# One DRAM row per token and choice for the expert results, in place of accumulating scatters

## The reference

```
scores = softmax(x @ Wg.T)                       # 16 experts
topi = the best 4 experts out of the best 2 of 4 groups
y = sum over the 4 chosen e of scores[e] * (silu(x @ W1[e].T) * (x @ W3[e].T)) @ W2[e].T
z = (silu(x @ Ws1.T) * (x @ Ws3.T)) @ Ws2.T      # shared expert
out = x_residual + y + z
```

## Time and profile before

| | |
|---|---|
| median of 3 runs | 1341.67 us (1340.03 to 1342.01) |
| the profiled execution | 1353.53 us, span 1351.8 us |
| PE busy | 1150.4 us, 85% of the span |
| DVE, POOL, ACT busy | 876.2 us, 688.8 us, 541.6 us |
| granted TensorE clock, mean | 0.936 |
| DMA traffic | 169.84 MB, mean 126 GB/s |
| expert loop of FFN f, of FFN h | about 460 to 651 us, about 1119 to 1317 us |
| seam after FFN f | about 651 to 760 us |
| end after FFN h | 1317 to 1351.8 us |

### The profile page before, as it was taken

One profiled execution on the slowest core, in us unless ns is written; L12 is line 12 of the kernel. 1 busy time (PEld: TensorE's weight loads), 2 busy tenths in 40 slices (PEclk: granted clock), 3 DMA queues, 4 the chain that ended last, 5 costly groups with the idle time before them and its releaser, 6 DMA issues.

```text
span 1351.8 us, 26055 instructions
## 1 busy us (share of the span) xinstructions
PE 1150.4 (85%) x8706; PEld 615.6 (46%) x8706; DVE 876.2 (65%) x2067; ACT 541.6 (40%) x846; POOL 688.8 (51%) x841
## 2 busy tenths in 40 slices
PE   6888999998898899999287899999879878899990
PEld 2343444442654556566144344444247445565650
DVE  5578898991674345555389799999667524354543
ACT  2124777779520122222032477777844011222210
POOL 4352344444036577767453355454520656667671
PEclk9887999999988999999689899999998988899995
DMA  4424333320824679887745322121053347788868
GB/s 140 147 86 126 111 116 120 109 65 3 287 83 131 183 164 161 151 159 108 191 138 169 117 57 58 55 60 52 3 211 87 108 149 180 133 148 157 156 87 262
DMA packets 145875, 169.84 MB, mean 126 GB/s; under 512 B 20240, under 2 KB 130768, under 8 KB 145232
## 3 DMA queue, kind: packets, MB, share of 16 engines
q1 hardware_dynamic: 115856, 128.79, 32.8%
q0 software_dynamic: 29184, 38.36, 16.8%
q10 hardware_dynamic: 704, 1.02, 0.2%
HBM read 93.29 MB, written 76.18 MB: 125 GB/s over the span
## 4 chain that ended last, share of the span: by engine, by line
PE 57%; DVE 18%; DMA 7%; issue 6%; ACT 6%; SPq 2%; another core or an unknown queue 2%; POOL 2%; POOLq 0%; ACTq 0%; DVEq 0%
PE pair_ps L1992 10%; PE o_ps L1757 9%; ACT arena L845 4%; DVE nm L1119 4%; PE pair_ps L2025 4%; DMA x_slots<-y_sb,slot_i 4%; DVE bm L1119 3%; PE pair_ps L2028 2%; PE t_ps L1783 2%; PE pair_ps L1707 2%; PE pair_ps L1588 2%; PE pair_ps L1687 2%; PE pair_ps L1999 2%; PE pair_ps L1712 2%
## 5 line engine op out<-in xcount | busy, mean ns | idle before, releaser
L845 ACT ACTIVATE arena<-pair_ps 128x1024 f32<-128x1024 f32 x320 | 322.8, 1024 | 131.0 <-PE pair_ps L1682 76.1
L625 POOL TENSOR_SCALAR_AFFINE_SELECT arena<-arena 128x512 f32<-128x512 f32 (+1 forms) x320 | 174.9, 547 | 240.9 <-ACT arena L845 240.4
L1119 DVE TENSOR_REDUCE nm<-pair_ps 128x2 f32<-128x1024 f32 (+1 forms) x192 | 232.6, 1222 | 33.4 <-PE pair_ps L1731 29.6
L685 POOL DMA_INDIRECT x_slots<-y_sb,slot_i x128 | 123.9, 968 | 168.4 <-DVE slot_i L1317 89.9
L1757 PE MATMUL o_ps<-arena 128*9 128x512 f32 (+7 forms) x2048 | 177.0, 441 | 4.1 <-POOL arena L625 3.9
L1992 PE MATMUL pair_ps<-arena 128*128 x512 | 167.7, 469 | 2.4 <-ACT arena L896 2.4
L1119 DVE TENSOR_REDUCE bm<-pair_ps 128x8 f32<-128x1024 f32 x128 | 155.4, 1218 | 4.2 <-PE pair_ps L1731 1.0
L701 POOL DMA_INDIRECT y_h<-xnT,dest x80 | 125.3, 1566 | 53.5 <-DVE xnT L1476 25.2
L701 POOL DMA_INDIRECT y_f<-xnT,dest x80 | 124.6, 1558 | 44.6 <-issue 20.5
L1459 DVE TENSOR_TENSOR arena<-arena,pair_ps 128x128 f32<-128x128 f32 x144 | 41.4, 288 | 124.7 <-ACT arena L901 70.0
L1992 PEld LDWEIGHTS pair_ps<-arena 128*128 128x128 f32 x512 | 93.7, 194 | 43.6 <-issue 6.0
(11 more groups left out here) (275 smaller groups left out, 1999.7 us busy)
## 6 DMA issues: line engine op xcount, KB each, us to landing
arena<-x_slots SPq DMA_DIRECT2D x128, 132.5 KB
arena<-in_w SPq DMA_DIRECT2D x4, 2816.0 KB, 18.6
arena<-q_a SPq DMA_DIRECT2D x64, 96.0 KB
arena<-q_b SPq DMA_DIRECT2D x64, 96.0 KB
y_f<-hw SPq DMA_DIRECT2D x11, 512.0 KB, 2.9
y_h<-hw SPq DMA_DIRECT2D x11, 512.0 KB, 2.9
arena<-in_w SPq DMA_DIRECT2D x2, 2048.0 KB, 17.2
arena<-y_f SPq DMA_DIRECT2D x8, 512.0 KB
```

Of the source, the lines that this page charges most:

```text
L625: pool.affine_select(p, p, pattern, ALU.is_ge, 0.0, base=0, channel_multiplier=-1)\
L685: pool.indirect_dma_start(x_slots, bass.IndirectOffsetOnAxis(ap=slot_i[:, t, k:k + 1], axis=0), y_sb[:, t, :], None).then_inc(sm(f"scat{n ...
L845: act.activation(p_ring[:, U % RING, :], pair_ps[:, pair_at("T", n, u)].rearrange("p a c -> p (a c)"), ACT.Exp, scale=SCALE).then_inc(sm(" ...
L1119: dve.tensor_reduce(dst, src, X, ALU.max, negate=not 2 <= u < 4).then_inc(sm("t_max_done"), 1)
```

## The change

- There is one DRAM tensor for each FFN, `y_rows[f]`, with a row for each pair of token and choice (8192 rows of 256 floats) and 1024 spare rows for padding. A result tile is scattered by one plain indirect DMA, with no `compute_op`. The wait for the scatter three before and the second scatter of a mixed tile are gone: 72 scatters in each FFN.
- A row of `x_slots` carries four destination rows in place of one token number (268 floats in place of 265). `where` reads weight and destination by one multiplication and one reduction, in four DVE instructions per four tiles in place of six and more.
- `store_x` and the 22 clearing DMAs are gone; only the clearing of the empty slots stays. The residual stays in `x_sb`.
- Behind the loop SP loads the four rows of each token, two tiles (1 MB, runs of 4 KB) a DMA: 8 DMAs with 8.4 MB, before 12 with 6.3 MB. The last two reuse the buffer of the first two and wait until DVE has summed tiles 0 to 3.
- `dve_sum` adds the four rows of two tiles and `x_sb` in three instructions: 1024, 512 and 512 elements per partition. `pool_back` is gone, so DVE does all of it.
- The output is stored in eight pieces of 256 KB.

```diff
-ACCS = 3
+Y_ROWS = ROWS * TOPK + P * XR
...
-            def store_x(b):
-                sp.wait_ge(sm("e_z_free"), TB * (b + 1) + past(f, NT))
-                sp.dma_start(y_acc[f][0][b * T:(b + 1) * T, :].rearrange("(t p) e -> p t e", p=P),
-                             x_sb[:, b * TB:(b + 1) * TB, :]).then_inc(sm("acc_x"), 16)
...
-            sp.wait_ge(sm("store_second"), 16 * MIXED * (1 + past(f, 1)))
+            rows = y_rows[f][0:ROWS * TOPK, :].rearrange("(t p k) e -> p t k e", p=P, k=TOPK)
             for b in range(B):
-                for a, to in ((0, x_sb), (1, back), (2, back2)):
-                    rows = y_acc[f][a][b * T:(b + 1) * T, :].rearrange("(t p) e -> p t e", p=P)
-                    sp.dma_start(to[:, b * TB:(b + 1) * TB, :], rows).then_inc(sm(f"load{2 * b + a % 2}"), 16)
+                if b == B - 1:
+                    sp.wait_ge(sm(f + "_x"), TB)
+                for u in (0, 2):
+                    sp.dma_start(back[b][:, u:u + 2], rows[:, b * TB + u:b * TB + u + 2])\
+                        .then_inc(sm(f"load{2 * b + u // 2}"), 16)
...
-            for b in range(B):
-                sp.wait_ge(sm("h_x"), (b + 1) * TB)
-                sp.dma_start(out_d[:, b * TB:(b + 1) * TB, :], x_sb[:, b * TB:(b + 1) * TB, :]).then_inc(sm("stored"), 16)
+            for t in range(0, NT, 2):
+                sp.wait_ge(sm("h_x"), t + 2)
+                sp.dma_start(out_d[:, t:t + 2, :], x_sb[:, t:t + 2, :]).then_inc(sm("stored"), 16)
...
             def result_out(j):
                 pool.wait_ge(sm("e_dest"), j // 4 + 1 + past(f, NJ // 4))
                 pool.wait_ge(sm("e_y_ev"), j + 1 + past(f, NJ))
-                if j == 0:
-                    pool.wait_ge(sm("acc_x"), 16 * B * (1 + past(f, 1)))
-                scatter_out(outs.index((j, 0)))
-                if j in MIX:
-                    scatter_out(outs.index((j, 1)))
+                pool.indirect_dma_start(y_rows[f], bass.IndirectOffsetOnAxis(ap=dest[:, j:j + 1], axis=0),
+                                        yt[:, j % XR, :], None).then_inc(sm(f"store{j % XR}"), 16)
...
+        def dve_sum(dve, f, q):
+            b, u, t = q // 2, q % 2 * 2, 2 * q
+            done = q + 1 + past(f, 2 * B)
+            part = back[b][:, u:u + 2]
+            dve.wait_ge(sm(f"load{q}"), 16 * (loads(q) + past(f, loads(q))))
+            dve.tensor_tensor(part[:, :, 0:2, :], part[:, :, 0:2, :], part[:, :, 2:4, :], ALU.add).then_inc(sm("back_half"), 1)
+            dve.wait_ge(sm("back_half"), done)
+            dve.tensor_tensor(part[:, :, 0, :], part[:, :, 0, :], part[:, :, 1, :], ALU.add).then_inc(sm("back_sum"), 1)
+            dve.wait_ge(sm("back_sum"), done)
+            dve.tensor_tensor(x_sb[:, t:t + 2, :], x_sb[:, t:t + 2, :], part[:, :, 0, :], ALU.add).then_inc(sm(f + "_x"), 2)
```

More of the change, by code:

```diff
@@ L185, in build @@
         y_flat = y_sb[:, :, :].rearrange("p t e -> p (t e)")
-        back = arena[:, o_p:o_p + NT * E].rearrange("p (t e) -> p t e", t=NT)
-        back2 = arena[:, o_p + NT * E:o_p + 2 * NT * E].rearrange("p (t e) -> p t e", t=NT)
+        back = [part.rearrange("p (u k e) -> p u k e", u=TB, k=TOPK) for part in
+                (arena[:, o_p:o_p + T * 8], arena[:, o_p + T * 8:o_p + T * 16], y_flat[:, 0:T * 8], arena[:, o_p:o_p + T * 8])]
         sil = sb("sil", [P, 2, T])
@@ L226, in build @@
         k_d = {s: nc.dram_tensor("k_" + s, (B, BLOCKS[s] - 2, 3, P, T), BF16).ap() for s in "ab"}
-        y_acc = {f: [nc.dram_tensor(f"y_{f}{a}", (ROWS + 4 * P, E), F32).ap() for a in range(ACCS)] for f in "fh"}
+        y_rows = {f: nc.dram_tensor(f"y_{f}", (Y_ROWS, E), F32).ap() for f in "fh"}
         pair_ps = ctx.enter_context(nc.psum_tensor("pair_ps", [P, RINGP, 2, 512], F32))
@@ L245, in build @@
         o += 16
-        nowhere = c_f[:, o:o + XR]
-        rows_i = c_f[:, o + XR:o + XR + NT]
-        o += XR + NT
+        rows_i = c_f[:, o:o + NT * TOPK].rearrange("p (t k) -> p t k", t=NT)
+        nowhere = c_f[:, o + NT * TOPK:o + NT * TOPK + XR]
+        o += NT * TOPK + XR
         lane, lane_late, lane_unit = c_f[:, o:o + 1], c_f[:, o + 1:o + 2], c_f[:, o + 2:o + 3]
@@ L499, in sp_ffn_slots @@
             sp.wait_ge(sm("e_order"), 1 + past(f, 1))
-            for b in range(B - 1):
-                store_x(b)
             sp.wait_ge(sm("padded"), 16 * NE * (1 + past(f, 1)))
@@ L637, in pool_combine @@
             pool.tensor_tensor(osq[:, n % 2], yv, yv, ALU.mult).then_inc(sm("b_sq"), 1)
-        def pool_back(pool):
-            pool.wait_ge(sm("back_sum"), TB)
-            for t in range(TB, NT):
-                if t % TB == 0:
-                    for q in (2 * (t // TB), 2 * (t // TB) + 1):
-                        pool.wait_ge(sm(f"load{q}"), 16 * loads(q))
-                pool.tensor_tensor(back[:, t, :], back[:, t, :], back2[:, t, :], ALU.add).then_inc(sm("back_sum"), 1)
         def pool_out_bias(pool, t):
@@ L653, in pool_out_bias, with pool_k_ones @@
             pool.tensor_tensor(x_sb[:, t, :], x_sb[:, t, :], bo[:], ALU.add).then_inc(sm("a_bo"), 1)
+        def pool_k_ones(pool):
+            pool.memset(arena2[:, 16 * T // 2:], ONES2).then_inc(sm("k_ones"), 1)
         def pool_attn(pool, s):
-            pool.memset(arena2[:, 16 * T // 2:], ONES2).then_inc(sm("k_ones"), 1)
             for b in range(B):
@@ L732, in _ @@
             pool.wait_ge(sm("a_ones"), 1)
+            pool_k_ones(pool)
             pool_attn(pool, "a")
             pool_ffn(pool, "f")
-            pool_back(pool)
             vo = v_all.rearrange("p g t (h c) -> p g t h c", h=2)
@@ L1228, in dve_seam, with dve_back @@
                 dve_seam_rstd(dve, 1 if s == "a" else 3, a, c)
-        def dve_back(dve, f, t):
-            if t % TB == 0:
-                for q in (2 * (t // TB), 2 * (t // TB) + 1):
-                    dve.wait_ge(sm(f"load{q}"), 16 * (loads(q) + past(f, loads(q))))
-            if f == "h" or t < TB:
-                dve.tensor_tensor(back[:, t, :], back[:, t, :], back2[:, t, :], ALU.add).then_inc(sm("back_sum"), 1)
-                dve.wait_ge(sm("back_sum"), t + 1 + past(f, NT))
-            else:
-                dve.wait_ge(sm("back_sum"), t + 1)
-            dve.tensor_tensor(x_sb[:, t, :], x_sb[:, t, :], back[:, t, :], ALU.add).then_inc(sm(f + "_x"), 1)
-            if f == "f":
-                dve.wait_ge(sm("f_x"), t + 1)
-                dve_stats(dve, 2, t)
+        def dve_sum(dve, f, q):
[8 more added lines that the diff above has]
+            dve.tensor_tensor(x_sb[:, t:t + 2, :], x_sb[:, t:t + 2, :], part[:, :, 0, :], ALU.add).then_inc(sm(f + "_x"), 2)
+        def dve_back(dve, t):
+            if t % 2 == 0:
+                dve_sum(dve, "f", t // 2)
+                dve.wait_ge(sm("f_x"), t + 2)
+            dve_stats(dve, 2, t)
         def dve_ffn(dve, f):
@@ L1537, in _ @@
             dve_ffn(dve, "h")
-            for t in range(NT):
-                dve_back(dve, "h", t)
+            for q in range(2 * B):
+                dve_sum(dve, "h", q)
         def pe_turn(pe, s, b, u):
```

81 lines of the change are left out of this document (23 added, 58 removed).

## The result

The change took 1390.63 us (median of 4 runs, 1371.99 to 1406.57) beside 1340.85 us before (4 runs, 1337.96 to 1342.01): 1.026 of before, 95% interval 1.019 to 1.034. I had forecast 1337.0 us and a range of 1327.0 to 1345.5. The sign was wrong, and the range missed it by 45 us.

What follows compares the result with a forecast made beforehand. PE was taken to bound the expert loops, DVE the seam, DMA and DVE the end. Start of the loops -1.5, seam -0.9 and end -2.3 made -4.7 us: 1348.8 profiled, 1337.0 us for the median, range 1327.0 to 1345.5.

Steps and rivals of the forecast that it cites:

- start of the loops: Start of the expert loops: without the fourth store, loads of tiles 4 and 5 come sooner; -1.5 us in f, 0 in h.
- Rival A: Expert loops: heavy DMAs cause the stalls seen in loop h, half of them go, -6 us more, 1331 us; chance 0.22.
- my account of the loop: Expert loop: it follows PE, which hides cheaper scatters, fewer `where` instructions and less DMA traffic, so these are worth nothing.
- tail behind the loop, f and h: Behind each expert loop: the last scatters start and land sooner, so SP's first load comes 4.2 us (f), 4.3 us (h) earlier.
- first issue to first sum, f: First landing behind loop f: the first sum waits for 1.05 MB in place of 1.57, 5.1 us after issue, -1.7 us.
- a sum of two tiles, at the end: DVE's three adds for two tiles: 1.2 + 0.69 + 0.69 = 2.6 us; eight of them at the end take 20.8 us.
- end of loop f to first L999, seam of block b: Seam behind loop f: tail, landing and unstretched DVE instructions outweigh longer sums, so the first L999 comes 6.0 us earlier.
- seam behind the first load, to the scatters of h: Seam on DVE between the FFNs: -0.9 us with its tail, bounds -2.6 and +1.7; longer sums against less stretching by POOL.
- end, from the first load: Last loads, sums and output stores: 29.1 us against 27.1 before, +2.0, on a start 4.3 us earlier, so -2.3.
- Rival C: Seam: POOL's contention goes on, the relief of 4.4 us fails and stretched adds cost 3.8 more; +3.5, 1345.2 us; chance 0.14.
- rival B: Loads at the end stay at 350 GB/s, so the end is +0.8 in place of -2.3; 1340.1 us; chance 0.10.
- Rival D: Landing and stores give nothing: plain scatters land as late as accumulating ones, PE's wait at the start stays; 1340.1 us; chance 0.09.

Runs made afterwards that it cites:

- before_row268: Kernel before with rows of 268 in place of 265 floats, the extra ones repeating the token's row: 1331.13 us (0.999) without stalls, 1403.77 us (1.029) with stalls.
- change_again: The change itself, unaltered, measured again beside the kernel before in a session without stalls: 1316.75 us, 0.987 of before.

## Why the prediction was wrong, and where it was right

**The step that failed.** "Cheaper scatters, fewer DVE instructions in `where` and less DMA traffic lie beside PE there and are worth nothing, as long as PE's work hides them" was argued from the loop and tacitly used for the stage in front of it. Apart from the -1.5 us for the fourth store, the scatter phase was not in the sum, in either direction, and the wider row was not costed. In the measurement that the forecast was held against, this stage cost 41.9 us (23.6 in f, 18.3 in h) and the loops behind it 10.9. The runs show both sides of it:

Without stalls the stage is bound by the scatters. The page of the change (second session), chain that ended last, by line:

```profile
PE pair_ps L1943 11%; PE o_ps L1708 9%; DMA x_slots<-y_sb,slot_i 8%; ACT arena L806 4%; DVE nm L1080 4%; PE pair_ps L1976 4%; DVE bm L1080 3%; PE pair_ps L1979 3%; PE t_ps L1734 2%; PE pair_ps L1658 2%; PE pair_ps L1638 2%; PE pair_ps L1663 2%; PE pair_ps L1950 2%; PE pair_ps L1539 2%; PE pair_ps L1633 2%
```

8% of the span is a wait for scatters into x_slots, as in seven other profiles without stalls (10 to 12% in the three with pauses, none listed for three in flight), and 4% in the profile that I predicted from. PE is through with the shared expert and waits for rows, here the kernel before with rows of 268 floats and the change:

```profile
451.77 0.66 PE L1967 MATMUL t_ps<-c_f,arena 128*128 128x128 f32 x2 [7.24 <-DMA arena<-x_slots]
```

```profile
448.68 0.41 PE L1918 MATMUL t_ps<-c_f,arena 128*128 128x128 f32 x2 [3.06 <-DMA arena<-x_slots]
```

"The first three stores end before PE is through with the shared expert, so they go at nothing; DVE and PE hide them" is the mis-sized term: no engine is seen waiting for the stores, but the scatters beside them end later, and the loop's first loads wait for the scatters. I had priced the start of the loops at -1.5 us. By the stages of profiles without stalls (the kernel with rows of 268 floats, 84.6 / 81.9, against the change, 78.9 / 79.7) it is -7.9, from one execution each in two sessions; by the times of one session the stores are worth 3.4 us in the kernel before and 6.0 in the change. In my trace of before its own stalls (ACT waited 9.57 and 9.99 us at 422.21 and 432.80) kept PE in the shared expert nearly until the rows had come, so that it waited for them only 1.02 and 0.44 us; a sign was there, the 4% in its chain, and I passed over it.

With stalls the sign turns. Rival A had the evidence, and read it backwards: it took POOL's alternating late and accumulating scatters for the cause and expected lighter DMAs to shrink the stalls. They did not shrink with the DMA load: the DMA share from 420 to 440 us is 0.34 in the change and was 0.49 before, and the stalls are twice as long. With three scatters in flight, 48 in place of 43 in 62 us, they grew again. In the loops too: without stalls each takes 173.3 us from first to last result (`before_row268`), in my trace of before 179.1 and 186.5, in the change with stalls 187.7 and 188.8. I had written that changed stalls in loop h would show my account of the loop to be wrong; what was wrong is that they belong to the loop at all, since they come and go with the session.

**What held.** Term by term, from profiles without stalls (`before_row268` for before, `change_again` for the change):

| step | forecast | measured |
|---|---|---|
| tail behind the loop, f and h | -4.2, -4.3 | -4.2 (9.14 to 4.98), -4.2 (9.18 to 5.01) |
| first issue to first sum, f | 6.8 to 5.1 | 6.9 to 5.1 |
| a sum of two tiles, at the end | 2.6 | 2.70 (21.57 / 8) |
| end of loop f to first L999, seam of block b | -6.0 | -7.4 |
| seam behind the first load, to the scatters of h | +3.3 | +3.1 |
| end, from the first load | +2.0 | +2.2 (+2.8, -0.6) |
| start of the loops | -1.5 | -7.9 |
| loops | 0 | 0.0, +0.4 |

The second to fourth rows are parts of the others and don't count in the sum. +3.3 is the seam's -0.9 less its tail of -4.2. The rest of the difference of the two spans, 1327.1 and 1317.0, is 0.4 ahead of the first scatter. The sum is -10.1; the ratios say -12 to -17 us, so up to 7 us lie in the spread between profiled executions and sessions, which I did not resolve. One slip in the working: 2.7 us for 1.05 MB fits neither rate (2.6 at 402 GB/s, 3.0 at 350); the 5.1 us measured show that it did no harm.

Rows of the change (first profile), the end of loop f on POOL and SP, then the seam on DVE, which answer to the earlier trace rows:

```profile
686.11 0.96 POOL L671 DMA_INDIRECT y_f<-xnT,dest  x1 [0.30 <-issue]
...
687.69 3.51 POOL L634 MEMSET arena<- 128x4096 f32 x1
...
688.58 2.17 SPq L520 DMA_DIRECT2D arena<-y_f  x4
```

```profile
693.60 1.23 DVE L1198 TENSOR_TENSOR arena<-arena 128x1024 f32<-128x1024 f32 x1 [8.92 <-DMA arena<-y_f]
694.86 0.69 DVE L1200 TENSOR_TENSOR arena<-arena 128x512 f32<-128x512 f32 x1
...
713.52 0.17 DVE L913 TENSOR_SCALAR nw<-nw 128x4 f32<-128x4 f32 x1
...
719.21 1.47 DVE L1198 TENSOR_TENSOR y_sb<-y_sb 128x1024 f32<-128x1024 f32 x1
...
721.80 1.46 DVE L1202 TENSOR_TENSOR x_sb<-x_sb,y_sb 128x512 f32<-128x512 f32 x1
```

The last scatter lands 2.47 us after its start, the memset runs while DVE waits for loads, and L913 takes 0.17 us (2.69 before). Rival C's mechanism is there, in four adds of batch 2 (1.47, 0.98, 1.46 and 1.53 us where 1.23 and three times 0.69 are usual), and small: 2 us. The loads at the end, a window of the change that answers to the last of the earlier trace rows:

```profile
1378.00:1400.00 22.00, 18.48 (x22) 0.50 1.03 409
```

409 GB/s settles rival B: the long runs of 4 KB give the rate of the weights (402), and not 350. The Trainium skill (DMA: Bandwidth & Descriptors, Where 436 GB/s comes from) has 358 GB/s as a core's share of the memory; the measurement stands above it, and the measurement decides. Rival D falls with the 2.47 us.

**What stays open.** What a stall is. Shown: it comes in some sessions and not in others, on the same chip; it holds ACT, DVE and SP with their inputs there, even SP's register steps, and PE waits for them; in the shared expert it ends with POOL's run of scatters; three scatters in flight in place of two make it worse (1402 to 1427 us in one session). That POOL's scatters cause it is argued from this and from the timing; the edit that would test it, pauses in a session with stalls, met no such session. Why the change loses more than the kernel before has two accounts, and each has one run: the wide row alone takes 1.029 of before (interval from 1.006, 1.014 by all runs) with 44 scatters in place of 39, and the missing stores alone take 1.015 (1.008 to 1.022) with 39. How much of the change's loss each makes is open, and plain scatters in place of accumulating ones were not tried apart. Why a row of 1072 bytes lets scatters follow sooner is not known, nor what differs between the sessions; no run controlled what else the chip was doing.

**A version that beats both?** Without stalls, three scatters in flight (0.982) beat the kernel before and the change (0.987 in the same session). With stalls it is the worst of all (1.064). No version measured here is ahead in both: with stalls the kernel before, as it stands, is the fastest.

## What to carry to other kernels

A stage whose cover you name must be read in a profile that is typical: this one took 11.86 us more than the median. Its span is 24.7 us above that of `before_row268`, of which 19.0 lie in the expert loops, 4.8 in the two stages; its waits for "remote" were the sign of it, and they half hid that the scatters bound the loop's start. When a change touches how densely POOL issues indirect DMAs, look at what other engines do at that time, and measure in several sessions: the same edit gained 7 us in one and lost 25 in another. A plain store for which nobody waits can still cost (3.4 to 6.0 us for eight here), where scatters move beside it and somebody waits for their landing.

## What was unexpected of the hardware

During dense indirect DMAs of POOL (0.96 us of every 1.3 to 1.4), ACT can stand still for 10 to 43 us with its inputs ready, DVE can fall to one small instruction every 1.4 us in place of every 0.2, and a register step of SP that takes 22 ns otherwise takes up to 707. In other sessions the same program shows none of it (the change, 1317 and 1402 us), and on one chip a kernel had none in one session and had them in another (`before_row268`, 1331 and 1404 us). A memset of POOL (3.51 us) holds a DVE instruction of four elements until it ends (2.96 us in place of 0.17).
